# Batching four key tiles per exponential in the global-row attention of a two-layer transformer kernel on eight cores

## What is computed

```python
qb = q.reshape(b, h, nb, bs, dh)          # h = 16 heads, bs = 64, dh = 64
gq = qb[:, :, global_indices]
row_scores = jnp.einsum('bhgqd,bhkd->bhgqk', gq, k) * scale      # scale = 1/8
out_rows = jnp.einsum('bhgqk,bhkd->bhgqd', jax.nn.softmax(row_scores, axis=-1), v)
...
final = out_local + out_gk
final = final.at[:, :, global_indices].set(out_rows)
```

## Time and profile before

| | |
|---|---|
| time, median of 2 runs | 5071.36 us (5070.88 to 5071.84) |
| time of the profiled execution | 5112.67 us |
| its span on the slowest core (core 6) | 5111.1 us |
| spans of the 8 cores in it | 5052.2 to 5111.1 us |
| TensorE busy, core 6 | 2721.6 us (53%) |
| VectorE busy, core 6 | 1595.1 us (31%) |
| ScalarE busy, core 6 | 877.2 us (17%) |

### The profile page before, as it was taken

The page is one execution under the profiler, slowest core; times in us unless marked ns, Lnnn a source line. Parts: engine busy times, 40 slices in busy tenths (PEclk is TensorE's granted clock), DMA queues, the critical chain, the costliest instruction groups (busy, mean ns, idle before and its releaser), DMA issues. The chain is left out here.

```text
span 5111.1 us, 48167 instructions; the slowest of 8 cores (5052.2 to 5111.1 us)
## 1 busy us (share of the span) xinstructions
PE 2721.6 (53%) x16028; PEld 1360.8 (27%) x16028; DVE 1595.1 (31%) x3289; ACT 877.2 (17%) x1580; POOL 288.2 (6%) x475
## 2 busy tenths in 40 slices
PE   2577787862999965555433333336104765004454
PEld 1234454542443422221122212224001222002222
DVE  4132211124111141112222222222855555463332
ACT  1013454511101010000122222220101232000000
POOL 0200000010201101000000000001000000110000
PEclk9875555565998866666555555557556776557777
DMA  2100000013725401110000000001052001541112
GB/s 78 27 4 1 1 1 1 1 17 50 71 28 58 42 1 13 13 13 9 5 1 1 1 1 1 1 1 17 0 99 54 37 37 40 80 66 33 33 33 82
DMA packets 186076, 134.41 MB, mean 26 GB/s; under 512 B 108016, under 2 KB 163312, under 8 KB 183792
## 3 DMA queue, kind: packets, MB, share of 16 engines
q0 software_dynamic: 147200, 97.70, 13.3%
q1 hardware_dynamic: 38640, 33.64, 2.1%
HBM read 187.02 MB, written 25.17 MB: 42 GB/s over the span
## 5 line engine op out<-in xcount | busy, mean ns | idle before, releaser
L556 PE MATMUL g1hp<-b4q1T,b4tern 128*128 128x512 bf16 x1024 | 302.0, 467 | 215.3 <-ACT b4hsp L574 124.8
L1537 PE MATMUL a0sb<-b1qTa,b1kTa 17*128 17x128 bf16 x2176 | 341.2, 301 | 1.7 <-PEq L1454 1.7
L1551 PE MATMUL a0yp<-b1vaug,b1Bp 128*128 128x65 bf16 x2176 | 225.1, 236 | 120.3 <-DVE b1Bp L1624 46.3
L1609 ACT ACTIVATE b1Bp<-a0sb 128x512 bf16<-128x512 f32 x384 | 229.3, 597 | 308.0 <-PE a0sb L1537 228.7
L207 PE MATMUL f0gps<-b2lnT,b2wg 128*128 128x512 bf16 x768 | 195.5, 413 | 62.2 <-DMA b2wu<-f0wu 60.9
L1624 DVE TENSOR_TENSOR b1Bp<-b1Bp,b1tril 128x128 bf16<-128x128 bf16 x256 | 57.3, 225 | 542.8 <-ACT b1Bp L1604 541.2
L556 PEld LDWEIGHTS g1hp<-b4q1T,b4tern 128*128 128x128 bf16 x1024 | 115.5, 115 | 401.4 <-issue 332.1
L1551 PEld LDWEIGHTS a0yp<-b1vaug,b1Bp 128*128 128x128 bf16 x2176 | 136.4, 117 | 255.9 <-issue 254.9
L1537 PEld LDWEIGHTS a0sb<-b1qTa,b1kTa 17*128 17x128 bf16 x2176 | 183.8, 124 | 39.3 <-issue 2.1
L214 PE MATMUL f0ups<-b2lnT,b2wu 128*128 128x512 bf16 x768 | 191.8, 408 | 0.0
L247 PE MATMUL f0dps<-b2wd,b2hT 128*128 128x512 bf16 x768 | 185.4, 410 | 3.4 <-PEq L185 3.4
(11 more groups left out here) (793 smaller groups left out, 4148.1 us busy)
## 6 DMA issues: line engine op xcount, KB each, us to landing
b4big<-g1w POOLq DMA_DIRECT2D x16, 1024.0 KB, 9.7
hs_scr<-b4hsp POOLq DMA_DIRECT2D x32, 512.0 KB, 2.9
b4big<-g1w POOLq DMA_DIRECT2D x64, 256.0 KB, 4.0
b4big<-hs_scr SPq DMA_DIRECT2D x64, 256.0 KB, 4.6
b2wg<-f0wg POOLq DMA_DIRECT2D x48, 256.0 KB, 4.9
b2wu<-f0wu POOLq DMA_DIRECT2D x48, 256.0 KB, 5.5
xs<-x SPq DMA_DIRECT2D x1, 8192.0 KB, 28.4
xo<-xs SPq DMA_DIRECT2D x1, 8192.0 KB, 23.1
```

The lines of the kernel that those rows point to most:

```text
L556: mm = t.matmul(hp[:, c % 2, n4 * 512:(n4 + 1) * 512], t1v[:, j, c * 128:(c + 1) * 128], q1T[:, j, n4 * 512:(n4 + 1) * 512], start=(j == 0 ...
L1537: t.matmul(sbat[:, gb % 2, jj * 128:(jj + 1) * 128], kT[hb:hb + 17, oc, j * 128:(j + 1) * 128], qT[hb:hb + 17, oc, i * 128:(i + 1) * 128], ...
L1551: mm = t.matmul(yps[:, h, 0:65], Bp[:, gb % 2, jj * 128:(jj + 1) * 128], v_aug[:, j, 65 * h:65 * h + 65], start=(k == 0 and jj == 0), stop ...
L1609: s.activation(Bp[:, gb % 2, 0:128 * nj], sbat[:, gb % 2, 0:128 * nj], AF.Square).then_inc(ph_s, 1)
```

## The change

The row block's 32 steps become 8 (`idx`), each of four key tiles of one head. In a step TensorE issues four S matmuls into four neighbouring 64-column pieces of one PSUM bank, ScalarE turns all 256 columns into probabilities with one instruction, and TensorE issues four A matmuls. The first four steps are head 0 of the pair, the last four head 1 (`h2 = idx // 4`). The double buffers stay, with 256 columns instead of 64 in each half; the probabilities are now `pr4`, another view of the same scratch tile. Semaphores count one per step of four.

```diff
-        BRS, BRP, BRA = 32 * g_, 32 * g_, 32 * g_
+        BRS, BRP, BRA = 8 * g_, 8 * g_, 8 * g_
+        pr4 = scr9[:, 0:1024].rearrange("pp (a b) -> pp a b", a=2)
...
-                for i in range(32):
-                    h2, tc = i % 2, i // 2
+                for idx in range(8):
+                    h2, sup = idx // 4, idx % 4
                     base = 64 * h2
-                    if i >= 2:
-                        t.wait_ge(rp_s, BRP + i - 1)
-                    t.matmul(rsp[:, i % 2, 0:64],
-                             kT[base:base + 64, g_, tc * 128:(tc + 1) * 128],
-                             qT[base:base + 64, g_, 0:64],
-                             start=True, stop=True).then_inc(rs_s, 1)
-                    t.wait_ge(rp_s, BRP + i + 1)
                     h = 2 * g_ + h2
-                    t.matmul(ryp[0:64, h2, 0:65], pr[:, i % 2, :],
-                             v_aug[:, tc, 65 * h:65 * h + 65],
-                             start=(tc == 0), stop=(tc == 15)).then_inc(ra_s, 1)
+                    if idx >= 2:
+                        t.wait_ge(rp_s, BRP + idx - 1)
+                    for t4 in range(4):
+                        tc = 4 * sup + t4
+                        mm = t.matmul(rsp[:, idx % 2, 64 * t4:64 * t4 + 64],
+                                      kT[base:base + 64, g_,
+                                         tc * 128:(tc + 1) * 128],
+                                      qT[base:base + 64, g_, 0:64],
+                                      start=True, stop=True)
+                    mm.then_inc(rs_s, 1)
+                    t.wait_ge(rp_s, BRP + idx + 1)
+                    for t4 in range(4):
+                        tc = 4 * sup + t4
+                        mm = t.matmul(ryp[0:64, h2, 0:65],
+                                      pr4[:, idx % 2, 64 * t4:64 * t4 + 64],
+                                      v_aug[:, tc, 65 * h:65 * h + 65],
+                                      start=(sup == 0 and t4 == 0),
+                                      stop=(sup == 3 and t4 == 3))
+                    mm.then_inc(ra_s, 1)
...
-                for i in range(32):
-                    s.wait_ge(rs_s, BRS + i + 1)
-                    if i >= 2:
-                        s.wait_ge(ra_s, BRA + i - 1)
-                    s.activation(pr[:, i % 2, :], rsp[:, i % 2, 0:64], AF.Exp,
-                                 scale=0.125).then_inc(rp_s, 1)
+                for idx in range(8):
+                    s.wait_ge(rs_s, BRS + idx + 1)
+                    if idx >= 2:
+                        s.wait_ge(ra_s, BRA + idx - 1)
+                    s.activation(pr4[:, idx % 2, 0:256], rsp[:, idx % 2, 0:256],
+                                 AF.Exp, scale=0.125).then_inc(rp_s, 1)
...
-                v.wait_ge(ra_s, BRA + 32)
+                v.wait_ge(ra_s, BRA + 8)
```

## The result

| | before | after |
|---|---|---|
| median | 5076.16 us (10 runs) | 4929.68 us (11 runs) |
| lowest | 5070.60 us | 4902.07 us |
| ratio after/before | | 0.9702, 95% interval 0.9668 to 0.9736 |
| span of the slowest core, profiled execution | 5111.1 us | 4918.6 us |

The interval means 2.6% to 3.3% less time. One of the 11 runs after, 5021.47 us, was slow, with one die of the chip at a lower granted clock; it is left out of the ratio, and the median of the other ten is 4924.9 us. The forecast was 4925 us, 2.9% less.

What follows compares the result with a forecast made beforehand. The prediction took the row blocks to be bound by latency of TensorE-ScalarE turns. Cutting 32 turns to 8 shortens each block from 30.8 to 12.5 us, 146 us for eight: 5071.4 - 146 = 4925 us, range 4901 to 4964.

Steps and rivals of the forecast that it cites:

- What bounds it: Head-pair loop's row blocks: TensorE and ScalarE take turns, 0.92 us per step, 30.8 us per block, with no engine the bound.
- The exponential of 256 columns at 0.38 us: ScalarE in the row block: one wide exponential takes 0.38 us against 0.22 for 64 columns, adding 0.16 per turn.
- Further matmuls 0.053 us apart: TensorE in each turn: three further score and three further value matmuls add 0.16 us per group; bounds 0.03 to 0.13 apart.
- The worry about weights of 64 columns: Value matmuls: spacing was read from weights of 128 columns, ours have 64; bounds 0.03 or 0.13 us apart.
- The turn of 1.40 us and the block of 12.5: Row block: a turn of four tiles takes 1.40 us against 0.92, a block 12.5 us against 30.8.
- The sum of 146 us: Eight row blocks, each 18.3 us shorter, all on the path: 146 us saved.
- Carried over to the median: The 146 us taken unchanged off the timed runs' median: 5071.4 - 146 = 4925 us.
- No overlap of matmuls: Rival in the row block: each further matmul costs weight load and full duration, turn 3.15 us, kernel 5037 us; chance 0.03.
- The clock rises in the denser block: Rival in the row block: denser TensorE work lifts the clock above 1.2 GHz, saving 19 us more, 4906 us; chance 0.06.
- Slower through the stages behind: Rival: output projection (up to 76 us) and last feed-forward net (up to 484 us) lose clock; chance 0.02.
- Off the path: Rival: the row blocks don't set the span, for example something shared holds the slowest core; 5071 us, chance 0.02.

Runs made afterwards that it cites:

- early issue: Against the kernel before, one tile per step, TensorE's next score matmul issued ahead of the waiting value matmul: median 4960.75 us, ratio 0.9781.

## Why the prediction was right

*What bounds it.* Latency of turns, not an engine. Right: the same exponentials in fewer turns kept 16.7 of 18.3 us per block, and the same instructions in another order, with two turns under way at once, saved 14 us.

*The exponential of 256 columns at 0.38 us*, read from a row with 64 partitions. Right: 384 ns.

*Further matmuls 0.053 us apart.* Right for the changed kernel: four scores take 0.37 to 0.39 us and four value matmuls 0.40, against 0.39 expected for each. The worry about weights of 64 columns was empty: 0.40 with them, 0.38 with 128 in the earlier trace rows.

*The turn of 1.40 us and the block of 12.5.* Measured 1.40, and 12.5 or 12.6. The sum of 146 us in the loop is 145.7.

*Carried over to the median.* 5071.4 - 146 = 4925 against 4929.7 measured; by the later median of the kernel before, 5076.2, it would have been 4930. So close a hit of the median is in part luck: the executions after the change, the slow one aside, range from 4902 to 4964 us. What the working earned is the loop's 145.7. The profiled span alone would have misled: it fell by 192.5 us, and 52 of them belong to the first feed-forward net, which ran at another granted clock.

*The rivals.* No overlap of matmuls: fell, four take 0.4 us and not 1.2. The rule in the Trainium skill, page "TensorE: Matmul & The Clock Gate", section "Part 3: Packing small matmuls — row/col tiling", that weight loads overlap only matmuls on other rows, is not what the traces show: on the same rows each score matmul started 0.05 us after the one before, with its own weight load. There is a grain of it: on opposite halves of the rows they start 0.02 us apart, worth 6 us of the loop.

*The clock rises in the denser block*: fell. The granted clock of the loop after the change, core 6:

```profile
2430.00:3262.00 832.00, 283.76 (x3212) 172.72 (x3212) 255.02 (x880) 245.38 (x488) 0.00 (x0) 0.50 0.00 1
```

It is 0.50, the level of 1.2 GHz, as in the earlier trace rows. By the Trainium skill, page "TensorE: Matmul & The Clock Gate", section "Part 1: The HAM clock gate (the 'warmup' mystery)", sustained matmul activity releases the clock; the row blocks, at 12.5 us each and a granted clock of 0.50, didn't show it. One reading of this rival was off. It put TensorE's busy share in the new turns at 56%, but the score group starts before the value group has ended, and that time was counted twice. The windows of the block before (41%) and of five new turns (51%) are:

```profile
2576.20:2607.20 31.00, 12.72 (x64) 7.26 (x64) 0.03 (x1) 8.43 (x33) 0.00 (x0) 0.50 0.00 0
```

```profile
2534.00:2541.00 7.00, 3.60 (x40) 2.62 (x40) 0.00 (x0) 1.92 (x5) 0.00 (x0) 0.50 0.01 2
```

*Slower through the stages behind*: fell. From the output projection to the end it takes 1639.8 us, and 1639.7 before. The last 1511 us of the span, a window as long as that in the earlier trace rows, have the same mean clock:

```profile
3407.00:4918.00 1511.00, 580.30 (x2284) 242.69 (x2284) 753.97 (x1124) 128.76 (x72) 69.95 (x114) 0.66 0.22 50
```

*Off the path*: fell. Taking the blocks out altogether shortens the loop by 258 us, where 259 were read from the timeline.

The working came out so close because nothing ran beside the chain, as the kernel without row blocks shows. Every link could be read from a row of the same kernel, and a check was at hand: the links had to add up to the old turn of 0.92 us before a new one was built from them.

## What to carry to other kernels

Where two engines hand work to each other and both are mostly idle, measure one trip in the timeline, split it into its links, and count the trips; the busy times say little. Then carry more per trip (512 columns, one whole PSUM bank, was the most tried here) or put a second trip under way by issuing the next producer ahead of the waiting consumer, which needs a second buffer for what is handed over and no further instruction. The two add to each other: a block took 12.5 us with four tiles, 16.6 with early issue and 7.7 with both. It is not quite a product, which would be 12.5 x 16.6 / 30.8 = 6.7, since the start of a block, 1.7 to 2.0 us, is paid once in any case. To judge a change worth a few per cent, compare the length of the stage it touches between two fixed lines, since spans of whole executions also carry what the clock did elsewhere.

## What the runs showed of the hardware that I had not expected

Four exponentials of 64 columns back to back take 0.57 us, though one alone takes 0.22: each further one adds 0.12.

Score matmuls with 64 rows of weights start 0.05 us apart on the same rows of the array, in one PSUM bank or in two, and 0.02 us apart when they alternate between its halves ((0.29 - 0.23)/3).

The same stage of the same instructions, the first feed-forward net, took 597 us at a granted clock of 0.93 and 649 at 0.84 on core 6 in two executions. Why the clock differed there was not tried.
